# Value products of eight heads at once, the maxima's transposes in another PSUM bank, and a new order of prologue, pieces and end

## The reference, cut to what matters

```python
xq, xk, xv = x @ wq.T, x @ wk.T, x @ wv.T        # split into 32 heads of 16
xq, xk = rotary_pos_emb(xq), rotary_pos_emb(xk)
scores = jnp.where(causal, einsum('bqhd,bkhd->bhqk', xq, xk) * hd ** -0.5, NEG_INF)
out = einsum('bhqk,bkhd->bqhd', softmax(scores), xv).reshape(B, T, C)
x = _layernorm(x + out @ wo.T)
xf = x / 128.0
inter = silu(einsum('bsh,ih->bsi', xf, w_gate)) * einsum('bsh,ih->bsi', xf, w_up)
inter_q = trunc(clip(inter * 128.0, -128.0, 127.0)).astype(int8)
down = einsum('bsi,hi->bsh', inter_q.astype(float32), w_down)
x = _layernorm(x + trunc(clip(down * 128.0, -128.0, 127.0)).astype(int8))
```

## Time and profile before

| what | us |
| --- | --- |
| median of 3 runs | 416.82 (415.2 to 417.55) |
| the profiled execution | 418.91 |
| its span, first to last instruction | 417.1 |
| TensorE busy | 374.8 |
| DVE busy | 255.9 |
| ACT busy | 217.6 |
| POOL busy | 83.5 |

### The profile page before, as it was taken

The page is one execution under the profiler, slowest core; times in us unless marked ns, Lnnn a source line. Parts: engine busy times, 40 slices in busy tenths (PEclk is TensorE's granted clock), DMA queues, the critical chain, the costliest instruction groups (busy, mean ns, idle before and its releaser), DMA issues.

```text
span 417.1 us, 7212 instructions
## 1 busy us (share of the span) xinstructions
PE 374.8 (90%) x2532; PEld 289.0 (69%) x2532; DVE 255.9 (61%) x902; ACT 217.6 (52%) x355; POOL 83.5 (20%) x80
## 2 busy tenths in 40 slices
PE   7958866999999999978799988699999999999991
PEld 4746544777677776756577766488888888878880
DVE  5754865576667757694243526675555555548886
ACT  5866376766837677594344363345344444333331
POOL 3112012101303010352200100035233333111111
PEclk9989998999999999999899999599999999999997
DMA  8876758578570946949600040012222200000111
GB/s 279 294 118 136 145 84 138 65 155 113 79 132 13 164 97 119 198 52 229 137 2 8 6 152 1 2 50 77 77 75 72 65 32 8 24 2 27 67 60 50
DMA packets 79841, 37.60 MB, mean 90 GB/s; under 512 B 68672, under 2 KB 72896, under 8 KB 79808
## 3 DMA queue, kind: packets, MB, share of 16 engines
q1 hardware_dynamic: 76928, 35.08, 38.5%
q10 hardware_dynamic: 2880, 2.10, 2.5%
HBM read 17.24 MB, written 2.10 MB: 46 GB/s over the span
## 4 chain that ended last, share of the span: by engine, by line
PE 72%; DVE 8%; ACT 6%; DMA 5%; SPq 4%; issue 3%; POOL 1%; ACTq 0%; POOLq 0%; DVEq 0%
PE bank L832 8%; PE bank L834 6%; PE bank L833 6%; PE bank L968 5%; PE s_pair L832 4%; PE s_pair L833 4%; PE s_pair L834 4%; PE st_pair L833 4%; PE st_pair L832 4%; PE st_pair L834 4%; PE bank L1059 4%; PE bank L1060 4%; PE st_pair L949 3%; SPq L237 3%; DMA XR<-xT 3%
## 5 line engine op out<-in xcount | busy, mean ns | idle before, releaser
L631 DVE CUSTOM_DVE_ANT_0 SM<-s_pair,K 128x128 f32<-128x128 f32 (+1 forms) x256 | 76.2, 354 | 71.6 <-PE s_pair L935 71.6
L423 ACT ACTIVATE PTS<-st_pair 128x768 f32<-128x768 f32 x64 | 51.7, 809 | 44.0 <-PE st_pair L952 43.1
L319 POOL TENSOR_TENSOR RQ<-RQ,QS 128x256 f32<-128x256 f32 x32 | 21.9, 685 | 119.1 <-ACT QS L402 118.8
L545 ACT ACTIVATE f_a<-f_c 128x512 f32<-128x512 f32 x22 | 13.9, 632 | 59.6 <-DVE f_c L761 59.6
L832 PE MATMUL bank<-WQH,XH 128*128 128x512 f32 x88 | 38.6, 439 | 4.4 <-ACT V L394 4.4
L304 POOL TENSOR_TENSOR GL<-gu_raw,GH 128x1024 fp32r<-128x1024 f32 x11 | 26.6, 2417 | 78.2 <-ACT GH L466 78.2
L949 PE MATMUL st_pair<-identb,maskb 128*128 128x256 bf16 x128 | 35.8, 280 | 6.8 <-ACT PTS L423 6.6
L834 PE MATMUL bank<-WQH,XL 128*128 128x512 f32 x88 | 35.2, 400 | 0.0
L833 PE MATMUL bank<-WQL,XH 128*128 128x512 f32 x88 | 35.1, 399 | 0.0
L1059 PE MATMUL bank<-DH,IQ 128*128 128x512 f32 x88 | 34.4, 390 | 0.2 <-POOL DL L309 0.2
L1060 PE MATMUL bank<-DL,IQ 128*128 128x512 f32 x88 | 34.2, 389 | 0.0
(11 more groups left out here) (122 smaller groups left out, 880.8 us busy)
## 6 DMA issues: line engine op xcount, KB each, us to landing
gu_raw<-wgu SPq DMA_DIRECT2D x11, 512.0 KB, 4.5
w_raw<-wqkvo SPq DMA_DIRECT2D x6, 512.0 KB, 9.0
wd_raw<-wd SPq DMA_DIRECT2D x11, 256.0 KB, 3.2
RES<-x SPq DMA_DIRECT2D x4, 512.0 KB, 4.5
out<-o SPq DMA_DIRECT2D x8, 256.0 KB, 2.0
XR<-xT SPq DMA_DIRECT2D x3, 512.0 KB, 5.4
w_raw<-wqkvo ACTq DMA_DIRECT2D x4, 256.0 KB, 4.5
QT<-QS SPq DMA_TRANSPOSE x64, 3.7
```

The lines of the kernel that those rows point to most:

```text
L423: nc.scalar.activation(PTS[:, u:u + 2, :], st_pair[:, :, 0:SW], ACT.Exp, scale=-1.0).then_inc(S["pr"], 1)
L631: last = nc.vector.tensor_tensor_reduce(out=SM[:, half, cols], in0=s_pair[:, half, cols], in1=above, scale=1.0, scalar=HUGE, op0=ALU.add, ...
```

## The change

- **Octets.** The value product handles eight heads in sixteen matmuls, two groups of four behind each other, into the lower and the upper half of bank 2, every fourth step, 11 steps behind. ACT copies 512 columns at once. The ring PTS holds ten heads. The loop has 72 steps.
- **Turn bank.** The maxima's transposes go to bank 3 and are items of TURN, at steps 1, 5, 9 and 13 of a batch, ahead of that step's other item. They wait for the reader of the item before them, and the item behind them waits for ACT's copy of the maxima (`mt_c`). No value product or maximum waits for the other any more.
- **Prologue.** V of batch 1 goes to banks 2 and 3. The sine parts of batch 0 alternate between T1 and RES, so that a sine part waits for the rotation before the last. The order of sines, pieces, rotations and weight splits on ACT and DVE is new. As RES is used, the load of x into it moves in SP's queue from ahead of the first stack to behind the third.
- **Pieces.** The four tensors' pieces are made in four steps (1 to 4 and 9 to 12), one in each, where it was three; third pieces go up to step 5 and 13, the split of x to step 13 and 14.
- **Batch 3 and end.** The fourth transpose of y, gate 0 to up 1 start later; gate 2 takes the place of gate 3 in step 66, in bank 4, and is no longer evacuated early (EARLY = 2). Gate 3 is split around the end of the loop; up 2 lies between the transposes after it, up 3 in halves ahead of and behind the output products. On DVE the product silu(gate) x up of number 2 stands between the last residuals and the last layer norms.
- SM, which nobody reads, is bf16.

```diff
-LAG_ST, LAG_PV, LAG_M = 7, 10, 5
-STEPS = NP + LAG_PV - 1
-R_PTS = 8
-DENSE = [("proj", m, 0, (0, 1, 4, 5, 0, 1)[m], -1, 0) for m in range(6)] + [("proj", 4 + t, 1, t, -1, 0) for t in range(NT)]
+LAG_ST, LAG_PV, LAG_M = 7, 11, 5
+STEPS = NP + LAG_PV - 3
+R_PTS = 10
+DENSE = [("proj", m, 0, (0, 1, 4, 5, 0, 1)[m], -1, 0) for m in range(6)] + [("proj", 4 + t, 1, 2 + t, -1, 0) for t in range(NT)]
+OUT_STEPS = (("back", 0, 1), ("back", 1, 3), ("chan", 0, 5), ("back", 2, 9), ("back", 3, 11), ("chan", 1, 13))
...
-        DENSE += [("yt", 0, 0, 0, g, 1), ("yt", 1, 0, 1, g + 2, 1), ("yt", 2, 0, 0, g + 3, 1), ("yt", 3, 0, 1, g + 4, 1)]
-        DENSE += [(kind, n, 0, int(kind == "up"), g + 5 + 3 * n + (kind == "up"), 2) for n in range(3) for kind in ("gate", "up")]
+        DENSE += [("yt", 0, 0, 0, g, 1), ("yt", 1, 0, 1, g + 2, 1), ("yt", 2, 0, 0, g + 3, 1), ("yt", 3, 0, 1, g + 5, 1)]
+        DENSE += [("gate", 0, 0, 0, g + 7, 2), ("up", 0, 0, 1, g + 9, 2), ("gate", 1, 0, 0, g + 11, 2), ("up", 1, 0, 1, g + 12, 2)]
-        TURN += [(kind, n, b - 1, g + at) for kind, n, at in (("back", 0, 1), ("back", 1, 3), ("chan", 0, 5), ("back", 2, 9), ("back", 3, 11), ("chan", 1, 13))]
+    for at in range(PAIRS):
+        TURN += [("max", 0, (g + at - LAG_M) // 4, g + at)] if g + at >= LAG_M and at % 4 == LAG_M % 4 else []
+        TURN += [(kind, n, b - 1, g + at) for kind, n, t in OUT_STEPS if b and t == at]
-TURN += [("back", 0, B - 1, NP + 1), ("back", 1, B - 1, NP + 3), ("chan", 0, B - 1, NP + 5),
+TURN += [("max", 0, NO - 1, NP + 1), ("back", 0, B - 1, NP + 1), ("back", 1, B - 1, NP + 3), ("chan", 0, B - 1, NP + 5),
-GU_STEPS = (3 * PAIRS - 1, 3 * PAIRS + 1, 3 * PAIRS + 5, 3 * PAIRS + 7)
-EARLY = 3
+GU_STEPS = (3 * PAIRS - 1, 3 * PAIRS + 1, 3 * PAIRS + 8, 3 * PAIRS + 12)
+EARLY = 2
...
-        SM = sb("SM", [P, 2, SW], F32, ph1)
+        SM = sb("SM", [P, 2, SW], BF16, ph1)
...
+        def sine_part(n, m):
+            return RES[:, 0, :] if n == 0 and m % 2 else T1[:, :]
...
-            load_xn(0)
             for k in range(NO):
+                if k == 2:
+                    sp.wait_ge(S["rope"], 4)
+                    load_xn(0)
...
             for g in range(STEPS):
-                    for m in {1: [0], 2: [1, 2], 3: [3]}.get(s, []):
+                    for m in {1: [0], 2: [1], 3: [2], 4: [3]}.get(s, []):
-                    for m in {9: [0, 1], 10: [2], 11: [3]}.get(s, []):
+                    for m in {9: [0], 10: [1], 11: [2], 12: [3]}.get(s, []):
-                if b + 2 < B and s == 13:
+                if b + 2 < B and s == 14:
...
-                wait(act, "rope", n * 4 + m)
+                wait(act, "rope", n * 4 + m - (0 if n else 1))
...
-                nc.scalar.activation(MT[0:2 * OCT, g % 2, :], bAV[0:2 * OCT, T:T + P].bitcast(BF16), ACT.Copy).then_inc(S["mt_c"], 1)
+                nc.scalar.activation(MT[0:2 * OCT, g % 2, :], bTR[0:2 * OCT, 0:P].bitcast(BF16), ACT.Copy).then_inc(S["mt_c"], 1)
...
             def exps(p):
-                wait(act, "pv", (2 * p - R_PTS) // 4 + 1)
+                wait(act, "pv", (p - R_PTS // 2) // 4 + 1)
-            def pv_out(q):
-                act.wait_ge(S["pv"], q + 1)
-                n, g = divmod(q, H // 4)
-                wait(act, "ob", n * 4 - (NT if g < H // 8 else 0))
-                nc.scalar.activation(OT[:, g, :], bAV[:, 0:T], ACT.Copy).then_inc(S["ot"], 1)
+            def pv_out(o):
+                act.wait_ge(S["pv"], o + 1)
+                n, g = divmod(o, OCTS)
+                wait(act, "ob", n * 4 - (NT if g < OCTS // 2 else 0))
+                nc.scalar.activation(OT[:, 2 * g:2 * g + 2, :], bAV[:, :].rearrange("p (g t) -> p g t", g=2), ACT.Copy).then_inc(S["ot"], 1)
...
-            for m in range(4):
-                sine(0, m, DENSE[m][3])
-                if m == 0:
-                    w_hi(6)
-                    w_hi(7)
-                first_piece(0, 0, m)
-                if m == 1:
-                    x_hi(1)
-                if m:
-                    second_piece(0, 0, m - 1)
+            sine(0, 0, DENSE[0][3])
+            w_hi(6)
+            first_piece(0, 0, 0)
+            sine(0, 1, DENSE[1][3])
+            w_hi(7)
+            x_hi(1)
+            first_piece(0, 0, 1)
+            second_piece(0, 0, 0)
+            sine(0, 2, DENSE[2][3])
+            sine(0, 3, DENSE[3][3])
+            second_piece(0, 0, 1)
+            first_piece(0, 0, 2)
+            first_piece(0, 0, 3)
+            second_piece(0, 0, 2)
...
-                values(1, t, t)
+                values(1, t, 2 + t)
...
-                if g >= LAG_PV and g % 2 == 0:
-                    pv_out((g - LAG_PV) // 2)
+                if g >= LAG_PV and (g - LAG_PV) % 4 == 0:
+                    pv_out((g - LAG_PV) // 4)
...
-                if b + 2 < B and s == 12:
+                if b + 2 < B and s == 13:
...
-            silu(2, 2)
+            silu(2, 0)
...
-            for m in range(4):
-                rotate(0, m, DENSE[m][3])
-                if m == 0:
-                    w_lo(6)
-                    w_lo(7)
-                if m == 1:
-                    dve.wait_ge(S["xh"], 1)
-                    nc.vector.tensor_tensor(XL[1][:, :, :], XR[1][:, :, :], XH[1][:, :, :].bitcast(F32), ALU.subtract).then_inc(S["xl1"], 1)
-                if m:
-                    third_piece(0, 0, m - 1)
-            third_piece(0, 0, 3)
+            rotate(0, 0, DENSE[0][3])
+            w_lo(6)
+            rotate(0, 1, DENSE[1][3])
+            w_lo(7)
+            dve.wait_ge(S["xh"], 1)
+            nc.vector.tensor_tensor(XL[1][:, :, :], XR[1][:, :, :], XH[1][:, :, :].bitcast(F32), ALU.subtract).then_inc(S["xl1"], 1)
+            third_piece(0, 0, 0)
+            rotate(0, 2, DENSE[2][3])
+            rotate(0, 3, DENSE[3][3])
+            for m in range(1, 4):
+                third_piece(0, 0, m)
...
-                    for m in {3: [0, 1], 4: [2, 3]}.get(s, []):
+                    for m in {3: [0], 4: [1], 5: [2, 3]}.get(s, []):
-                    for m in {11: [0, 1], 12: [2, 3]}.get(s, []):
+                    for m in {11: [0], 12: [1], 13: [2, 3]}.get(s, []):
...
-            silu_up(2, 2, 2)
+            silu_up(2, 0, 2)
...
-                              "back": ("on", 4 * b + n + 1), "chan": ("ol", 2 * b + n + 1)}[name]
+                              "max": ("mt_c", b + 1), "back": ("on", 4 * b + n + 1), "chan": ("ol", 2 * b + n + 1)}[name]
...
+            def strips(dst, slot, k, which):
+                for c in which:
+                    last = weights_by_y(dst, slot, k, c, 0)
+                return last
...
-                if what == "back":
+                if what == "max":
+                    pe.wait_ge(S["mp"], m + 1)
+                    if m == 0:
+                        pe.wait_ge(S["v_sb"], 2 * NT)
+                    for t in range(NT):
+                        last = nc.tensor.transpose(bTR[0:2 * OCT, t * P // 2:(t + 1) * P // 2].bitcast(BF16),
+                                                   MP[:, m % 2, t, :, :].rearrange("p k h -> p (k h)"), identb[:, 0, :])
+                    last.then_inc(S["mt_t"], 1)
+                elif what == "back":
-                    pe.wait_ge(S["ot"], m * 2 * groups + (half + 1) * groups)
+                    pe.wait_ge(S["ot"], m * OCTS + (half + 1) * OCTS // 2)
...
-            def maxima(g):
-                pe.wait_ge(S["mp"], g + 1)
-                wait(pe, "ot", (4 * g + LAG_M - 1 - LAG_PV) // 2 + 1)
-                for t in range(NT):
-                    last = nc.tensor.transpose(bAV[0:2 * OCT, T + t * P // 2:T + (t + 1) * P // 2].bitcast(BF16),
-                                               MP[:, g % 2, t, :, :].rearrange("p k h -> p (k h)"), identb[:, 0, :])
-                last.then_inc(S["mt_t"], 1)
...
-            def pv(q):
-                b, g = divmod(q, H // 4)
-                wait(pe, "ot", q)
-                wait(pe, "mt_c", min((2 * q + LAG_PV - LAG_M) // 4 + 1, NO))
-                pe.wait_ge(S["pr"], 2 * q + 2)
+            def pv(o):
+                b, g = divmod(o, OCTS)
+                wait(pe, "ot", o)
+                pe.wait_ge(S["pr"], 4 * o + 4)
-                for key, to, blocks in ((0, slice(0, T), slice(0, 3, 2)), (1, slice(P, T), slice(1, 2))):
-                    for r in range(4):
-                        h = 4 * g + r
-                        probs = PTS[:, h % R_PTS, :].rearrange("p (k q) -> p k q", q=P)[:, blocks, :]
-                        last = nc.tensor.matmul(bAV[32 * r:32 * r + 32, to], V[:, b % 2, key, h, :], probs,
-                                                start=(key == 0), stop=(key == 1))
+                for quad in range(2):
+                    for key, at, n, blocks in ((0, 0, T, slice(0, 3, 2)), (1, P, P, slice(1, 2))):
+                        for r in range(4):
+                            h = OCT * g + 4 * quad + r
```

(31 more changed lines are left out.)

17 lines of the change are left out of this document (8 added, 9 removed).

## The result

| | median | lowest to highest | executions | profiled: time, span, mean clock |
|---|---|---|---|---|
| before | 417.19 us | 415.20 to 418.71 | 4 | 418.91, 417.1, 0.97 |
| after | 424.98 us | 421.48 to 426.77 | 4 | 424.78, 423.0, 0.95 |

The ratio is 1.018, 95% interval 1.010 to 1.026. The change makes the kernel slower by 7.8 us, where 409.7 had been predicted.

A forecast was written before the change was run, and what follows sets the result against it. TensorE, busy 374.8 of 417.1 us, was taken as the bound. Terms -2.5 + 1.9 - 8.0 + 2.1 + 0.4 - 1.0 = -7.1 took the profiled 418.9 to 411.8, or 409.7 as a median; range 403.0 to 415.5.

The forecast's parts named there:

- start and batch 0, to step 17: Prologue and batch 0: ACT's wait ends 0.6 earlier, ACT saves 1.1, value product 3 is already done (0.8): -2.5 us.
- batches 1 and 2, steps 17 to 48: From 73 to 170 us: octets save 1.9, new turn-bank stalls net +3.8; together +1.9 us (-3.0 to +4.5).
- steps 48 to 58: Batch 3, 170 to 210 us: later gates, fewer waits and products, less slow clock: -8.0 us (-10.5 to -4).
- rest of batch 3: Up to the first back transposes after the loop: 2.8 more for products, less 0.7 for switches: +2.1 us.
- end chain: After the loop: latency-set chain, products fit into its gaps, silu_up 2 costs about 0.4: +0.4 us (-0.5 to +1.5).
- clock at the end: Near 263 us: with six more products in the gap the clock falls later or not at all: -1.0 us.
- The stalls I wrote out: Batches 1 and 2: channel transposes wait 1.3, shifted scores of step 14 0.6, steps 4 to 6 0.5; 4.9 in all.
- The octet's own price: Value products, batches 1 and 2: one narrow-form entry and exit less saves 0.24 an octet, 1.9 for eight.
- The rivals: Turn bank free 404.8 (chance 0.20); tighter steps 48 to 57 413.7 (0.17); no difference 416.2 (0.10); slower 422.8 (0.08).
- The slower rival: Twelve maxima, batches 1 to 3: each shared turn-bank use becomes a TensorE, ACT, DVE hand-over, 1.5 each: 422.8 us; chance 0.08.

The follow-up runs named there:

- same fill in both: Three idle 512-column products in each of steps 9 to 16, added to the kernel before with the octet edit (420.38 us) and to the kernel before (416.13 us).
- before with fill: The kernel before with 24 idle products, three ahead of the shifted scores in each of steps 9 to 16: 416.13 us, ratio 0.999.

## Why the prediction was wrong, by its own steps

| step of the sum | predicted | change in the profile | what it was |
|---|---|---|---|
| start and batch 0, to step 17 | -2.5 | +1.0 | a moved wait, the octets and the clock |
| batches 1 and 2, steps 17 to 48 | +1.9 | +10.6 | two falls of the clock, a wait left out in each batch |
| steps 48 to 58 | -8.0 | -8.3 | right in direction, the size by luck |
| rest of batch 3 | +2.1 | +3.1 | within its bounds |
| end chain | +0.4 | -0.3 | right |
| clock at the end | -1.0 | -0.3 | the fall came again |

Against the profiled before, the sum of the steps was -7.1 and the span changed by +5.9. Of the miss of 13.0, 12.2 lie in the first two terms (3.5 and 8.7). The median misses by 15.3, because I took 2.1 off for a profiled before that was slower than its median, and the changed kernel's profiled execution (424.78) was not.

*Start.* The prologue did what was said: the gap before the value products of batch 1 is gone, and step 0 comes 4.6 us earlier. ACT's first piece was released at 56.60, 0.54 before, against -0.6 predicted. What I missed is that TensorE came there 3.2 us earlier (step 10), so the wait for that stack grew: ACT waited 3.19 (0.50 before) and TensorE 3.31 in step 11 (1.59 before). ACT and TensorE of the changed kernel, timeline:

```profile
56.60 0.84 ACT L410 ACTIVATE QS<-RQ 128x768 bf16<-128x768 f32 x1 [3.19 <-DMA QT<-QS]
...
58.29 0.37 PE L966 MATMUL st_pair<-identb,maskb 128*128 128x256 bf16 x1 [3.31 <-ACT PTS L431]
```

The window of the changed kernel behind it:

```profile
56.00:63.00 7.00, 4.71 (x46) 2.88 (x47) 1.04 (x5) 4.30 (x7) 1.34 (x2) 0.53 0.20 37
```

I had called ACT the bound from there to step 16 and costed its instructions, not TensorE's at half clock. With a wait of 3.3 in one place the clock was down from 56 to 63 us, and again from 70.5 to 74. Before had one such stretch in this part (68 to 71). With the prologue alone TensorE waits 3.82 there and 1.0 of the gain of 3.5 is left at step 17.

The octets failed in this term as well, where I had them save time. With them alone, and the old prologue, TensorE waits as long in step 11, and the growth to step 17 is 4.7:

```profile
62.88 0.27 PE L951 MATMUL st_pair<-identb,maskb 128*128 128x256 bf16 x1 [3.25 <-ACT PTS L426]
```

Idle products in these steps took 3.6 of those 4.7 away, so that was mostly the clock. No run holds it in batch 0 of the changed kernel itself; how its miss of 3.5 divides between wait and clock is not shown.

*Batches 1 and 2.* The stalls I wrote out were right in place and nearly in size: channel transposes 1.12 and 1.08 (1.3 predicted), shifted scores of step 14 0.55 and 0.55 (0.6). The reason was right too: behind the shifted scores of step 12, which end at 111.38, TensorE was ready after 2.7 us (2.6 said) and the copy done after 3.7 (3.9 said). Two steps failed. The sum left out OH: the copy of x had moved to step 13, ahead of it on ACT, so the output product waits 1.51 and 0.70. And it ended the price of a wait with the wait. The clock was a term at the end of the kernel alone, although the same page showed it falling behind waits. I also put these stalls down to the turn bank. By itself the bank costs nothing (416.6). It takes the pieces in step 12, which make ACT late, and the octets, which bring TensorE there early; with all pieces at their old steps the copy of the maxima is waited for nowhere. The code makes the channel transposes wait for that copy only because they share the bank, so the wait of 1.12 needs the bank too. No run has octets and pieces without it. My bounds of the term, -3.0 to +4.5, had no clock in them, and it came out 6.1 above them. That is the largest part of the 9.5 by which the time lies above the range; the start, at the very top of its own bounds (+1.0), adds to it.

*The octet's own price.* It came out as sized: the 32 records of one octet fill 1.44 us until the next product starts, and that one takes 0.34, so 1.55 with the exit, against 2 x (0.78 + 0.11) = 1.78 for two quads. That entering the narrow form costs 0.13 is still not separated by any row.

TensorE of the changed kernel, timeline:

```profile
251.22 1.51 PE L985 MATMUL bank<-PTS,V 128*32 128x256 f32 x32 [1.22 <-ACT PTS L431]
252.66 0.50 PE L844 MATMUL s_pair<-YH,GH 128*128 128x512 f32 x1
```

That saves 0.23 an octet. But from step 20 to 28, over two octets and with the old pieces, the runs with octets gain only 0.3, and a lump costs elsewhere: the value product above had to wait 1.22 (0.61 before), the wait for RES at the y transposes rose from 1.24 to 2.03, that for OL in batch 3 from 0.64 to 1.43. With the same fill in both, octets lose 4.3 us in all.

*Steps 48 to 58* gave -8.3 for -8.0, and the end part alone -9.6 in the profile, but -7.2 in the medians. Runs that change nothing there (prologue, turn bank, and before with fill) show -1.5, -3.5 and -2.5 in the same stretch. So the profiled execution of before was 1.5 to 3.5 us slow just there, and the true gain is about 5 to 7, 0.9 of it for the place in the octet. That this term matched to 0.3 is luck. I built -1.7 of clock and -2.4 of wait on one execution.

*The rivals.* The slower rival had 422.8 and thus nearly the time, but by a hand-over at every use of the turn bank; TensorE waited for ON once (0.5 us) in the changed kernel, and the run with the turn bank alone speaks against it. None of the rivals was the one that happened: short waits close together, then half speed.

Not settled: by what the pieces of steps 1 to 4 cost 3.3 us, of which the traces show 2.7 in three stretches, and why the clock falls behind the wait of 2.03 for RES in step 50 in three of six profiled executions, which makes the steps from 48 to 52 1.6 us longer.

## What to carry to other kernels

When TensorE is the bound and nearly full, price a new wait twice: its own length, and half of the stretch at 0.50 that may follow when several waits stand close together. Before moving a step on another engine, list what then stands ahead of the copies that TensorE waits for at that place, and try idle products in the waits: if they make the kernel faster, the clock is what you are paying. A part that saves work on the bound engine in larger lumps can lose it all to latency; test each part of a change alone before keeping the whole.

## What the hardware showed that was not expected

No single wait was long where the clock fell: 1.12, 0.55 and 1.51 us with products between them, 1.82 of 5.00 us busy, then 0.50. The octets alone had 0.56 and 0.69 us of waits in the same place and 1.00 throughout. Twenty-two products with no use, 5 us of work, made the changed kernel 6.9 us faster by the medians, 5.0 of it seen in the trace where they stand. And taking the maxima's transposes into the turn bank, twelve times in batches 1 to 3, cost nothing that can be measured by itself (ratio 1.0006). Nor does one wait decide alone: behind the same wait of 2.03 us for RES the clock fell in three executions of six.
